# Graph network kernel: node update with fp16 halves and a new order of the engines' steps, and a re-ordered GCN stage

## The chip, the cores and the metric

One core of one Trainium2 chip. The metric is the device time of one execution in microseconds (us). The kernel is written in Bass: every engine's instruction stream, its waits and its semaphores are written out by hand.

## What is computed

Four graph layers on 10,000 nodes of 512 features (x) with 2,500 edges, each behind a layer norm and relu and each added to x:

```
x = x + GCN(h)       # h = relu(layernorm(x)); 512 -> 128 -> 512, symmetric degree weights, self loops
x = x + SAGE(h)      # 3 sublayers: relu(h @ Wself + mean(h[src]) @ Wneigh + b), rows scaled to unit length
x = x + MPNN(h)      # the layer with the node update that is changed
x = x + SAGEConv(h)  # mean aggregation, batch norm over the nodes, relu
```

The third layer, with mish(z) = z * tanh(softplus(z)):

```
h        = mish([x[src], x[dst], edge_attr] @ W1 + b1)
messages = mish(h @ W2 + b2)
agg      = segment_sum(messages, dst)
u        = mish([x, agg] @ W3 + b3)
y        = x + u @ W4 + b4
out      = layernorm(y) * gamma + beta
```

## The kernel before, in words

The rows live in SBUF for the whole run, in 79 tiles of 128 rows ("slots"). Nodes that receive edges sit in the last 20 tiles (t = 59 to 78, "the zone"), so that only these meet messages. Activations that feed a product are kept as two fp16 halves (high and low part of a scaled fp32), turned so that features lie on the partitions. A product with fp16 halves takes three matmuls per 128 features: high by high weight, low by high weight, high by low weight. A product with fp32 operands takes one matmul per 128 features, which the trace shows as two records.

The stages run one after the other, with barriers between them:

- **prepare** (lines 228 to 702, 0 to 197 us of the span): sorts the edges, and splits each weight matrix into fp16 halves. The matrices stand in the dictionary `units` (line 133): for each, SyncE loads it, VectorE takes its largest absolute value (L590), ScalarE makes the high half (L439), VectorE the low half (L629), SyncE stores both (L343). Then come the bias parts (L646 to L652, L348) and last one large store of the selection matrices (L350), on whose landing the barrier waits.
- **gcn_layer** (lines 789 to 1221, 197 to 614 us) works on pairs of tiles in 55 steps of one shared schedule. `of_rows(s, lag, ...)` does rows pair g = s - lag: gather x (POOL L921), moments (VectorE L762), factors (POOL L772 to L780), normalise (ScalarE L785), turn (TensorE), project 512 to 128 (TensorE L1155), turn back (L1162), write the rows (VectorE L1020 or L1026). The zone's ten pairs come first. `of_end(s, lag, ...)` does end pair q = s - 10 - lag: product with Wlin (TensorE L1198), residual and moments (VectorE L1053, L762), factors again, normalise, turn, make halves (ScalarE L1120, VectorE L1061). For the last ten pairs, the zone's, it first gathers the edges' rows (POOL L955), passes a running sum from tile to tile (`carry`: VectorE copy L1035, TensorE L1171), builds a diagonal (VectorE L1043) and convolves (TensorE L1183, L1185; ScalarE L1107). Each engine's order within a step is the order of its `of_rows` and `of_end` lines. From step 10 on POOL also issues two indirect DMAs per step for slot numbers (L932, L937), from step 31 on three for sources (L944).
- three **sage_layer** calls, **edge_hidden**, then **edge_messages** (lines 1799 to 1930, 1822 to 1978 us): 20 tiles of messages; VectorE's `totals` (L1881) scales the aggregated product with W3's lower half and SyncE stores it for the node update.
- **node_update** (lines 1962 to 2253, 1980 to 2636 us): 79 tiles in 40 pairs, see below.
- **batch_rows** and **finish** (lines 2263 to 2458).

In the node update, step s of every engine holds work of three pairs. `whole_pair(v, lag, ...)` and `of_pair(v, lag, ..., which)` pick pair s - lag and the tiles of it:

- TensorE: `update` of pair s (L2217 adds b3 with a 3-row matmul, L2221 are the 48 matmuls of 256 columns), `second` of pair s-1 tile 0 (L2230 adds b4, L2234 adds x, L2239 are four fp32 products with W4, eight records), `turn` of pair s-2 (L222, eight transposes), `second` of pair s-1 tile 1.
- ScalarE: `next_rows` of s-2 (L743, relu of the norm), sigmoid, log, tanh of pair s (L2167, two instructions of 512 columns each; mish is written as z * tanh(-ln(sigmoid(-z)))), with the copies `hi` of s-2 (L2195) between log and tanh.
- VectorE: `residual` (L2132 and moments L716) and `y_stats` (L716) of s-1 and s-2, `add_messages` of pair s (L2101, zone only), `lo` (L2140), `times_z` (L2110, two of 512 columns, makes u).
- POOL: factors of both norms and `add_beta` (L2055). SyncE: loads and stores.

u (the buffers `uT`) is fp32 and double-buffered by pair. The wait that ties TensorE to the others is `pe.wait_ge(s_u, 2 * v.g + 2)` ahead of L2239.

## Time and profile before

| | us |
|---|---|
| median of 3 runs | 3074.97 (3073.33 to 3088.87) |
| the profiled execution | 3073.27 |
| its span, first to last instruction | 3071.0 |
| TensorE busy | 2573.3 (84%) |
| VectorE busy | 1851.7 (60%) |
| ScalarE busy | 1505.4 (49%) |
| POOL busy | 1221.5 (40%) |
| granted TensorE clock, mean | 0.950 of 2.4 GHz |

Busy times are averages over stages with different limits. Times in the rows below are from the start of the span. In a timeline row the columns are: start in us, time from the first start to the last end of the merged group in us, engine, line and operation, output from input, shapes, count, and in brackets the idle time before it with what ended it. "issue" means that the engine waited for nothing that the profile shows.

### The profile page before, as it was taken

To read this page: it belongs to the slowest core of one execution; us is meant where nothing else is said; L and a number is where in the kernel's file an instruction comes from. 1 tells how busy PE (TensorE), PEld (TensorE's weight loads), DVE (VectorE), ACT (ScalarE), POOL (GpSimd) and SP (SyncE) were. 2 spreads that over 40 slices of the span, in tenths; PEclk is the share of its full clock that TensorE was granted. 3 is DMA by queue.
4 is the path that set the end of the run, shared out by engine and by line. 5 is a ranking of instruction groups with operands and counts; after the bars stand their busy time and mean duration, and the time that the engine had idled before them with its cause. 6 is when DMAs were issued, how large, how long until landed. Compare 5 with 4: busy or idle time off the path is not lost. (4 is left out here: it accounts for less than half of the span.)

```text
span 3071.0 us, 44367 instructions
## 1 busy us (share of the span) xinstructions
PE 2573.3 (84%) x13170; PEld 1453.0 (47%) x13170; DVE 1851.7 (60%) x4344; ACT 1505.4 (49%) x2128; POOL 1221.5 (40%) x2065
## 2 busy tenths in 40 slices
PE   0347888789887999798979969799999999899964
PEld 0234554344443445344544547565555555444443
DVE  8744876578666876799864435345555566423333
ACT  7235665345333533355335756466666666332270
POOL 3666874236332332365545511133333333100146
PEclk9999998899998999899989989899999999999976
DMA  5154442278766887666553322322222234101268
GB/s 173 59 213 124 150 145 92 78 184 201 134 123 156 203 171 152 192 221 220 181 182 105 101 80 85 103 81 95 96 99 102 89 134 138 71 1 38 57 225 312
DMA packets 379160, 412.03 MB, mean 134 GB/s; under 512 B 198351, under 2 KB 237683, under 8 KB 376316
## 3 DMA queue, kind: packets, MB, share of 16 engines
q1 hardware_dynamic: 350364, 335.34, 37.0%
q0 software_dynamic: 28640, 74.78, 8.1%
q8 instruction: 78, 1.28, 0.2%
q14 instruction: 78, 0.64, 0.1%
HBM read 171.50 MB, written 197.28 MB: 120 GB/s over the span
## 5 line engine op out<-in xcount | busy, mean ns | idle before, releaser
L215 PE MATMUL s_ps_z<-s_w,slots 128*128 128x512 f16 x2844 | 645.7, 384 | 41.7 <-DMA s_bias<-in_L_gnn_b 41.7
L215 PEld LDWEIGHTS s_ps_z<-s_w,slots 128*128 128x128 f16 (+1 forms) x2844 | 280.9, 99 | 363.3 <-DMA s_bias<-in_L_gnn_b 43.1
L1571 ACT ACTIVATE s_g<-s_g,s_rn 128x512 f32<-128x512 f32 x237 | 170.0, 717 | 287.7 <-POOL s_rn L1461 287.7
L2239 PE MATMUL u_ps_o<-u_w,u_uT 128*128 128x512 f32 x632 | 288.6, 599 | 0.2 <-DVE u_uT L2110 0.2
L1461 POOL TENSOR_TENSOR s_rn<-s_em,minus_half 128x1 f32<-128x1 f32 x237 | 179.6, 758 | 253.0 <-DVE s_em L1515 245.1
L1500 DVE SCALAR_TENSOR_TENSOR s_g<-s_ps_z,s_f,s_bias 128x512 f32<-128x512 f32 x237 | 177.9, 751 | 140.3 <-PE s_ps_z L215 132.0
L2221 PE MATMUL u_ps_z<-slots,u_w 128*128 (+2 forms) x1920 | 236.7, 273 | 0.0
L2349 PE MATMUL z_ps_z<-slots,z_w 128*128 128x512 f16 (+1 forms) x960 | 211.7, 380 | 7.2 <-DMA z_w<-split_root 7.2
L2221 PEld LDWEIGHTS u_ps_z<-slots,u_w 128*128 128x128 f16 x1920 | 173.9, 98 | 37.7 <-issue 0.4
L716 DVE BATCH_NORM_STATS2 u_ny_st<-u_ps_o 128x6 f32<-128x512 f32 x79 | 54.7, 692 | 213.7 <-PE u_ps_o L2239 213.7
L743 ACT ACTIVATE u_h<-u_x,u_n_sh,u_n_rs 128x512 f32<-128x512 f32 x79 | 64.3, 814 | 229.3 <-POOL u_n_sh L738 229.3
L2239 PEld LDWEIGHTS u_ps_o<-u_w,u_uT 128*128 128x128 f32 x632 | 113.9, 190 | 113.7 <-issue 113.3
L1508 DVE SCALAR_TENSOR_TENSOR s_junk<-s_g 128x512 f32<-128x512 f32 x237 | 164.5, 694 | 4.1
L2167 ACT ACT_TABLE_LOAD x120 | 154.0, 1283 | 26.3 <-PE u_ps_z L2221 24.1
L215 PE MATMUL s_ps_z<-s_wn,s_aT 128*128 128x512 f16 x720 | 165.2, 379 | 0.0
L2318 DVE BATCH_NORM_STATS2 z_stats<-slots 128x6 f32<-128x512 f32 (+1 forms) x76 | 52.2, 687 | 185.7 <-ACT slots L2335 185.7
L743 ACT ACTIVATE s_h<-s_x,s_norm_sh,s_norm_rs 128x512 f32<-128x512 f32 x79 | 64.2, 813 | 176.0 <-POOL s_norm_sh L738 95.9
L2349 PEld LDWEIGHTS z_ps_z<-slots,z_w 128*128 128x128 f16 x960 | 94.6, 99 | 116.0 <-DMA z_w<-split_root 7.6
L2335 ACT ACTIVATE slots<-z_ps_z,bn_cols,z_f 128x512 f32<-128x512 f32 (+1 forms) x76 | 58.7, 772 | 158.3 <-PE z_ps_z L2349 158.2
L1292 POOL DMA_INDIRECT z_m<-h_rows,src_s x20 | 19.0, 950 | 257.1 <-DVE z_aT L1338 251.7
L215 PEld LDWEIGHTS s_ps_z<-s_wn,s_aT 128*128 128x128 f16 x720 | 70.4, 98 | 85.0
L1526 DVE SCALAR_TENSOR_TENSOR s_halves<-s_g,s_halves 128x512 f16<-128x512 f32 x158 | 108.0, 684 | 2.5 <-ACT s_halves L1559 2.5
(370 smaller groups left out, 5445.0 us busy)
## 6 DMA issues: line engine op xcount, KB each, us to landing
h_rows<-s_g SPq DMA_DIRECT2D x158, 256.0 KB
x_rows<-q_x SPq DMA_DIRECT2D x79, 256.0 KB
s_x<-x_rows SPq DMA_DIRECT2D x79, 256.0 KB
x_rows<-s_x SPq DMA_DIRECT2D x79, 256.0 KB
h_rows<-s_h SPq DMA_DIRECT2D x79, 256.0 KB
u_x<-x_rows SPq DMA_DIRECT2D x79, 256.0 KB
x_rows<-u_x SPq DMA_DIRECT2D x79, 256.0 KB
h_rows<-u_h SPq DMA_DIRECT2D x79, 256.0 KB
```

Source lines behind the costliest of these rows:

```text
L215: ins = nc.tensor.matmul(out_ap, a(c), w[:, part * size + c * n:part * size + (c + 1) * n], start=first and c == 0 and m == 0, stop=stop a ...
L743: return nc.scalar.activation(out_ap, in_ap, func, scale=self.rstd[b][:, 0:1], bias=self.shift[b][:, 0:1])
L1461: nc.gpsimd.tensor_tensor(out=rn[b][:, :], in0=em[b][:, :], in1=minus_half[:, :], op=POW).then_inc(s_rn, 1)
L1500: nc.vector.scalar_tensor_tensor(out=g[b][:, :], in0=ps_z[v.buf(4)][:, :], scalar=f[:, 0:1], in1=bias[:, :], op0=MUL, op1=ADD).then_inc(s_ ...
L1508: nc.vector.scalar_tensor_tensor(out=junk[:, :], in0=r[:, :], scalar=0.0, in1=r[:, :], op0=MAX, op1=MUL, accum_out=en[e][:, 0:1]).then_inc ...
L1526: nc.vector.scalar_tensor_tensor(out=part[:, D:2 * D], in0=g[v.buf(ng)][:, :], scalar=scale_out, in1=part[:, 0:D], op0=MUL, op1=SUB).then_ ...
L1571: nc.scalar.activation(g[b][:, :], g[b][:, :], ACT.Relu, scale=rn[v.buf(2)][:, 0:1]).then_inc(s_h, 1)
L2167: nc.scalar.activation(part, z if first else part, func, scale=scale, **kw).then_inc(sem, 1)
L2221: ins = nc.tensor.matmul(z, w3[:, at:at + P], pair_slots[:, :, part * D + k * P:part * D + (k + 1) * P], start=False, stop=k == C - 1 and ...
L2239: ins = nc.tensor.matmul(ps_o[b][:, :], ut_tile(v, c), w4[:, c * D:(c + 1) * D], start=False, stop=c == C - 1)
L2335: nc.scalar.activation(z_of(zx, g, c)[:, 0:n], ps_z[c][:, 0:n], ACT.Identity, scale=f[:, 0:1], bias=bn_cols[:, c:c + 1]).then_inc(s_z, 1)
L2349: ins = nc.tensor.matmul(out_ap, weights[:, at:at + P], a(k), start=first and k == 0 and m == 0, stop=stop and k == C - 1 and m == 2)
```

## The change

It splits W4 into fp16 halves like the other weights, and multiplies by them:

```diff
-    bias_d = dram("bias_parts", [3, 2 * D], BF16)
+    bias_d = dram("bias_parts", [3, D], BF16)
-    units = {"conv": (Wc, 1), "edge": (W1[0:2 * D, :], 2), "update": (W3[0:D, :], 1),
+    units = {"conv": (Wc, 1), "edge": (W1[0:2 * D, :], 2), "update": (W3[0:D, :], 1), "out": (W4, 1),
...
-                for k, v in enumerate((bl, gamma3, beta3)):
+                for k, v in enumerate((bl, gamma3, beta3, b3)):
```

In gcn_layer, epsilon is added by VectorE, the end pairs run one step later with four `cT` buffers, the zone's rows are scaled a second time when they are written, and the diagonal is gone:

```diff
-        def factors(self, pool, g, n, done, s_used, used, consts):
+        def above_eps(self, dve, g, n, done):
             b = g % 2
-            pool.wait_ge(self.s_mv, done)
-            nc.gpsimd.tensor_tensor(out=self.nm[b][:, 0:n], in0=self.mv[b][:, 0:n, 0], in1=minus_one2, op=MUL)
-            nc.gpsimd.tensor_tensor(out=self.ve[b][:, 0:n], in0=self.mv[b][:, 0:n, 1], in1=eps2, op=ADD).then_inc(
-                self.s_ve, 1)
+            dve.wait_ge(self.s_mv, done)
+            nc.vector.tensor_scalar(out=self.ve[b][:, 0:n], in0=self.mv[b][:, 0:n, 1], scalar1=LN_EPS, scalar2=None,
+                                    op0=ADD).then_inc(self.s_ve, 1)
+
+        def factors(self, pool, g, n, s_used, used, minus_one2, minus_half2):
+            b = g % 2
             pool.wait_ge(self.s_ve, g + 1)
+            nc.gpsimd.tensor_tensor(out=self.nm[b][:, 0:n], in0=self.mv[b][:, 0:n, 0], in1=minus_one2[:, 0:n], op=MUL)
...
-        FINISH = 3
+        FINISH = 4
...
                         ins.then_inc(s_rows, 1)
+                        dve.wait_ge(s_rows, g + 1)
+                        for k in range(2):
+                            e = 2 * g + k
+                            nc.vector.tensor_scalar(out=hwz[:, e * HID:(e + 1) * HID], in0=hw[g % 2][:, k * HID:(k + 1) * HID],
+                                                    scalar1=dis_dst[:, e:e + 1], scalar2=None, op0=MUL).then_inc(s_hwz, 1)
...
                 for s in range(STEPS):
-                    of_end(s, FINISH, lambda q: carry(q, 0))
-                    of_end(s, FINISH, lambda q: diagonal(q, 0))
-                    of_end(s, FINISH, lambda q: carry(q, 1))
                     of_end(s, FINISH + 2, lo)
                     of_rows(s, 0, lambda g: moments(g, 0))
                     of_rows(s, 2, rows_out)
                     of_rows(s, 0, lambda g: moments(g, 1))
-                    of_end(s, FINISH, lambda q: diagonal(q, 1))
                     of_end(s, FINISH, lambda q: residual(q, 0))
+                    of_end(s, FINISH - 1, lambda q: carry(q, 0))
                     of_end(s, FINISH, lambda q: residual(q, 1))
+                    of_end(s, FINISH - 1, lambda q: carry(q, 1))
...
-                        nc.tensor.matmul(out_ap, hwz[:, e * HID:(e + 1) * HID], diag[e % 2][:, :], start=True, stop=False)
+                        nc.tensor.matmul(out_ap, hwz[:, e * HID:(e + 1) * HID], ident[:, :], start=True, stop=False)
...
                     of_rows(s, 2, project)
-                    of_end(s, FINISH, lambda q: carry(q, 0))
                     of_rows(s, 1, lambda g: turn(g, 0))
                     of_end(s, FINISH, lambda q: convolve(q, 0))
                     of_rows(s, 1, lambda g: turn(g, 1))
-                    of_end(s, FINISH, lambda q: carry(q, 1))
                     of_rows(s, 2, rows)
                     of_end(s, FINISH, lambda q: convolve(q, 1))
                     of_end(s, FINISH, lambda q: linear(q, 0))
                     of_end(s, FINISH + 1, lambda q: turn1(q, 0))
                     of_end(s, FINISH, lambda q: linear(q, 1))
+                    of_end(s, FINISH - 1, lambda q: carry(q, 0))
                     of_end(s, FINISH + 1, lambda q: turn1(q, 1))
+                    of_end(s, FINISH - 1, lambda q: carry(q, 1))
```

edge_messages also takes the largest absolute message sum of each tile, and runs VectorE's loop unrolled:

```diff
+                    wait_count(dve, s_zmax, v.t - 1)
                     nc.vector.tensor_scalar(out=tot[b][:, :], in0=ps_g[b][:, :], scalar1=scale[:, 0:1],
                                             scalar2=None, op0=MUL).then_inc(s_tot, 1)
+                    dve.wait_ge(s_tot, v.t + 1)
+                    nc.vector.tensor_reduce(out=z_max[:, v.t:v.t + 1], in_=tot[b][:, :], op=MAX, axis=AX.X,
+                                            apply_absolute_value=True).then_inc(s_zmax, 1)
...
-                         (0, lambda v: mish.result(dve, r[:, :], v)), peel=8)
+                         (0, lambda v: mish.result(dve, r[:, :], v)), peel=ET, loop_end=ET)
```

In node_update some twenty small VectorE instructions and one small matmul at its start work out a power of two `g` for u from these maxima and b3. Then, per pair (`uT` is now one buffer, `u_hi` and `u_lo` are one fp16 buffer each, `unscale` is bf16; the three `step` functions below are those of VectorE, ScalarE and TensorE; `centred` is `y_stats` together with L2126, until now the first instruction of `residual`; `load_sigmoid_and_tanh` loads the one table set of ScalarE that holds both functions):

```diff
-                def times_z(k):
-                    def stage(v, tiles):
...
-                        nc.vector.tensor_tensor(out=part, in0=z, in1=part, op=MUL).then_inc(s_u, 1)
+                def times_z(v, tiles):
+                    for c in range(C):
+                        dve.wait_ge(s_th, mish_count(v, c // 2))
+                        part = chunk(uT, c, tiles)
+                        ins = nc.vector.scalar_tensor_tensor(out=part, in0=z_chunk(v, c, tiles), scalar=b3_cols[:, c:c + 1],
+                                                             in1=part, op0=ADD, op1=MUL)
+                        if c % 2:
+                            ins.then_inc(s_u, 1)
+                def lo_u(k):
+                    def stage(v, tiles):
+                        dve.wait_ge(s_uhi, mish_count(v, k))
+                        nc.vector.scalar_tensor_tensor(out=half(u_lo, k, tiles), in0=half(uT, k, tiles), scalar=g[:, 0:1],
+                                                       in1=half(u_hi, k, tiles), op0=MUL, op1=SUB).then_inc(s_ulo, 1)
+                    return stage
-                def y_stats(v):
+                def centred(v):
...
                 def step(v):
-                    of_pair(v, 2, residual, (1,))
-                    of_pair(v, 0, add_messages(0))
-                    of_pair(v, 0, add_messages(1))
-                    of_pair(v, 1, y_stats, (0,))
+                    of_pair(v, 1, centred, (0,))
+                    whole_pair(v, 0, times_z)
+                    whole_pair(v, 0, lo_u(0))
+                    whole_pair(v, 0, lo_u(1))
                     of_pair(v, 1, residual, (0,))
+                    of_pair(v, 1, centred, (1,))
+                    of_pair(v, -1, add_messages(0))
+                    of_pair(v, -1, add_messages(1))
                     of_pair(v, 2, lo)
-                    whole_pair(v, 0, times_z(0))
-                    whole_pair(v, 0, times_z(1))
-                    of_pair(v, 1, y_stats, (1,))
+                    of_pair(v, 1, residual, (1,))
...
+                def sigmoid(k):
+                    def stage(v, tiles):
+                        z_there(v, k)
+                        wait_count(act, s_ulo, mish_count(v, k) - 2)
+                        for c in (2 * k, 2 * k + 1):
+                            ins = nc.scalar.activation(chunk(uT, c, tiles), z_chunk(v, c, tiles), ACT.Sigmoid,
+                                                       scale=minus_f[:, 0:1], bias=minus_b3[:, c:c + 1])
+                        ins.then_inc(s_s, 1)
+                    return stage
+                def tanh(v, tiles):
+                    load_sigmoid_and_tanh(act)
...
+                def hi_u(v, tiles):
+                    wait_count(act, s_mm4, v.t)
+                    for k in range(2):
+                        act.wait_ge(s_u, mish_count(v, k))
+                        nc.scalar.activation(half(u_hi, k, tiles), half(uT, k, tiles), ACT.Copy,
+                                             scale=g[:, 0:1]).then_inc(s_uhi, 1)
                 def step(v):
-                    of_pair(v, 2, next_rows)
-                    whole_pair(v, 0, sigmoid)
+                    whole_pair(v, 0, sigmoid(0))
+                    of_pair(v, 2, next_rows, (0,))
+                    whole_pair(v, 0, sigmoid(1))
                     whole_pair(v, 0, log)
+                    whole_pair(v, 0, tanh)
+                    of_pair(v, 2, next_rows, (1,))
+                    whole_pair(v, 0, hi_u)
                     of_pair(v, 2, hi)
-                    whole_pair(v, 0, tanh)
...
-                        nc.tensor.matmul(z, b3_rows[:, c * P:(c + 1) * P], ones3[:, 0:tiles * P], start=True, stop=False)
...
-                    pe.wait_ge(s_u, 2 * v.g + 2)
+                    pe.wait_ge(s_uhi, 2 * v.g + 2)
+                    for part in range(2):
+                        for c in range(C):
+                            nc.tensor.matmul(ps_o[b][:, :], chunk_of_tile(u_hi, v, c),
+                                             w4[:, part * cols["out"] + c * D:part * cols["out"] + (c + 1) * D],
+                                             start=False, stop=False)
+                    pe.wait_ge(s_ulo, 2 * v.g + 2)
                     for c in range(C):
-                        ins = nc.tensor.matmul(ps_o[b][:, :], ut_tile(v, c), w4[:, c * D:(c + 1) * D],
+                        ins = nc.tensor.matmul(ps_o[b][:, :], chunk_of_tile(u_lo, v, c), w4[:, c * D:(c + 1) * D],
                                                start=False, stop=c == C - 1)
                 def step(v):
                     whole_pair(v, 0, update)
-                    of_pair(v, 1, second, (0,))
+                    of_pair(v, 1, second)
                     of_pair(v, 2, turn)
-                    of_pair(v, 1, second, (1,))
```

POOL's step becomes y_factor tile 0, add_beta, h_factors tile 0, y_factor tile 1, h_factors tile 1, all of pair s-1.

## Rows read from the trace of the kernel before

**Rows 1.** Windows: busy us of each engine, TensorE clock, DMA share, GB/s

```profile
2100.00:2600.00 500.00, 500.00 (x2923) 296.65 (x2922) 287.74 (x656) 315.97 (x404) 188.79 (x439) 1.00 0.31 107
290.00:420.00 130.00, 113.39 (x527) 68.23 (x528) 102.49 (x278) 90.43 (x150) 106.75 (x196) 1.00 0.48 148
530.00:614.00 84.00, 59.41 (x228) 30.95 (x226) 47.07 (x124) 29.95 (x54) 25.27 (x50) 0.85 0.23 79
```

**Rows 2.** Waits from 2100 to 2600 us: total us, times, longest

```profile
DVE u_ny_st L716 <- PE u_ps_o L2239: 169.1, 31, 6.2
```

**Rows 3.** Timeline of the node update, TensorE, one step of a pair

```profile
2304.44 0.28 PE L2217 MATMUL u_ps_z<-u_ones,u_b_rows 3*128 3x256 bf16 x1
...
2306.28 1.48 PE L2221 MATMUL u_ps_z<-slots,u_w 128*128 x12
...
2310.95 0.39 PE L2230 MATMUL u_ps_o<-u_b_rows,u_ones 3*128 3x512 bf16 x1
...
2311.72 3.65 PE L2239 MATMUL u_ps_o<-u_w,u_uT 128*128 128x512 f32 x8
...
2315.21 1.04 PE L222 MATMUL u_ps_t<-ident,u_h 128*128 128x128 f32 x8
...
2316.18 0.39 PE L2230 MATMUL u_ps_o<-u_b_rows,u_ones 3*128 3x512 bf16 x1
...
2320.54 0.28 PE L2217 MATMUL u_ps_z<-u_ones,u_b_rows 3*128 3x256 bf16 x1
```

**Rows 4.** Timeline of batch_rows, TensorE, fp16 matmuls of 512 columns

```profile
2699.76 16.57 PE L2349 MATMUL z_ps_z<-slots,z_w 128*128 128x512 f16 x76
```

**Rows 5.** Timeline of the node update, ScalarE

```profile
2312.66 1.26 ACT L2167 ACTIVATE u_uT<-u_ps_z,u_minus_f 128x512 f32<-128x512 f32 x2
...
2313.94 1.28 ACT L2167 ACT_TABLE_LOAD   x1
...
2315.24 1.34 ACT L2167 ACTIVATE u_uT<-u_uT,floor_col 128x512 f32<-128x512 f32 x2
...
2316.48 1.06 ACT L2195 ACTIVATE slots<-u_ps_t 128x512 f32 x2
...
2318.85 1.15 ACT L2167 ACTIVATE u_uT<-u_uT 128x512 f32<-128x512 f32 x2
...
2326.61 0.81 ACT L743 ACTIVATE u_h<-u_x,u_n_sh,u_n_rs 128x512 f32<-128x512 f32 x1 [5.16 <-POOL u_n_sh L738]
```

**Rows 6.** Timeline of the node update, VectorE

```profile
2301.41 0.75 DVE L2132 SCALAR_TENSOR_TENSOR u_x<-u_ps_o,u_ny_rs,u_x 128x512 f32<-128x512 f32 x1 [0.27 <-POOL u_ny_rs L2065]
...
2550.22 0.74 DVE L2101 TENSOR_TENSOR u_ps_z<-u_ps_z,u_zg 128x256 f32<-128x256 f32 x2
```

**Rows 7.** Timeline of prepare and of edge_messages, VectorE

```profile
94.54 24.75 DVE L590 TENSOR_REDUCE w_mx<-slots 128x1 f32<-128x512 f32 x11
...
176.95 4.68 DVE L629 SCALAR_TENSOR_TENSOR w_parts<-slots,up,w_parts 128x2048 f16<-128x2048 f32 x2 [2.73 <-ACT w_parts L439]
...
1882.72 1.12 DVE L1254 SCALAR_TENSOR_TENSOR n_total<-n_carry_w,n_carry_on,n_ps_a 128x128 f32<-128x128 f32 x4 [2.11 <-PE n_ps_a L1916]
```

**Rows 8.** Timeline of gcn_layer, POOL, one step with gathers

```profile
382.33 0.22 POOL L773 TENSOR_TENSOR q_norm_ve<-q_norm_mv,q_eps 128x2 f32<-128x2 f32 x1
382.63 0.72 POOL L777 TENSOR_TENSOR q_norm_rs<-q_norm_ve,q_minus_half 128x2 f32<-128x2 f32 x1
...
390.52 0.72 POOL L777 TENSOR_TENSOR q_norm_rs<-q_norm_ve,q_minus_half 128x2 f32<-128x2 f32 x1
```

**Rows 9.** Timeline of gcn_layer, VectorE, the zone's end pairs

```profile
514.07 0.17 DVE L1037 MEMSET q_m<- 1x128 f32 x1 [4.50 <-DMA q_m<-projection_rows,src_s]
...
569.66 0.26 DVE L1035 COPY q_m<-q_ps_t 1x128 f32<-1x128 f32 x1
...
580.81 0.26 DVE L1035 COPY q_m<-q_ps_t 1x128 f32<-1x128 f32 x1
...
588.88 0.26 DVE L1035 COPY q_m<-q_ps_t 1x128 f32<-1x128 f32 x1
```

More of the change, by code:

```diff
@@ L47 @@
 SIGMOID_FLOOR = 2.0 ** -80
+SIGMOID_AND_TANH = 2
 PEEL = 12
@@ L828, in gcn_layer @@
             sl = [sb(ctx, f"q_sel{b}", [P, P]) for b in range(4)]
-            diag = [sb(ctx, f"q_diag{b}", [P, P]) for b in range(2)]
             bias_row = x1[0][0:1, :]
@@ L2156, in _ @@
             def _(act):
-                act.wait_ge(s_f, 2)
-                def each_half(sem, before, func, scale, bias=None, first=False):
-                    def stage(v, tiles):
-                        b = v.j // 2
-                        for k in range(2):
-                            before(v, k)
-                            part = uT[b][:, k * D:(k + 1) * D].rearrange("p (c n) -> p c n", c=2)[:, :, 0:tiles * P]
-                            z = ps_z[b][k][:, :].rearrange("p (c n) -> p c n", c=2)[:, :, 0:tiles * P]
-                            kw = {} if bias is None else {"bias": bias}
-                            nc.scalar.activation(part, z if first else part, func, scale=scale, **kw).then_inc(sem, 1)
-                    return stage
+                act.wait_ge(s_f, 1)
@@ L2182, in _ @@
-                sigmoid = each_half(s_s, z_there, ACT.Sigmoid, minus_f[:, 0:1], first=True)
-                log = each_half(s_l, s_there, ACT.Ln, 1.0, bias=floor_col[:, 0:1])
-                tanh = each_half(s_th, l_there, ACT.Tanh, -1.0)
+                def sigmoid(k):
[7 more added lines that the diff above has]
+                    return stage
@@ new lines, in log @@
+                def log(v, tiles):
+                    for k in range(2):
+                        act.wait_ge(s_s, mish_count(v, k))
+                        nc.scalar.activation(half(uT, k, tiles), half(uT, k, tiles), ACT.Ln, scale=1.0,
+                                             bias=floor_col[:, 0:1]).then_inc(s_l, 1)
+                def tanh(v, tiles):
+                    load_sigmoid_and_tanh(act)
+                    for k in range(2):
+                        act.wait_ge(s_l, mish_count(v, k))
+                        nc.scalar.activation(half(uT, k, tiles), half(uT, k, tiles), ACT.Tanh, scale=-1.0).then_inc(s_th, 1)
```

233 lines of the change are left out of this document (130 added, 103 removed).

## The prediction

> **What bounds the kernel now.** The windows come first. In the node update TensorE is busy 500.00 of 500.00 us at full clock, while VectorE has 287.74, ScalarE 315.97 and POOL 188.79; in gcn_layer no engine is full (PE 113.39, DVE 102.49, ACT 90.43, POOL 106.75 of 130) and in its last part none is near (59.41 of 84, at clock 0.85) [rows 1]. The waits agree: what VectorE waits for in the node update is TensorE's L2239, 169.1 us in that window [rows 2]. So there TensorE's own work sets the time. The timeline gives it per pair: from one L2217 at 2304.44 to the next at 2320.54 is 16.10 us, made of the update 6.51, `second` 4.26, turn 0.97 and `second` 4.36 [rows 3]. In GCN the step is a chain through several engines.
>
> I sum against the profiled execution's own 3073.27 us, 1.7 below the median; the two stand for the same kernel.
>
> **Node update, TensorE.** In the update a chunk takes 6.51 / 4 = 1.63 us, its bias matmul included, while the 12 matmuls alone run from 2306.28 for 1.48 [rows 3]. Taking a last matmul of 0.27 off, 11 gaps make 1.21, so 0.11 each and 12 x 0.11 = 1.32. Without the bias a chunk saves 1.63 - 1.32 = 0.31, a pair 1.24, and the update is 5.27. In `second`, eight fp32 records fill the tile's end at 0.43 each = 3.44. They become 12 fp16 matmuls of 512 columns. The kernel has such a run elsewhere: 76 in 16.57 us, (16.57 - 0.38) / 75 = 0.216 each [rows 4], so 2.59; a tile saves 0.85. The pair step becomes 5.27 + 3.41 + 3.51 + 0.97 = 13.2. Over 40 updates and 79 seconds this is 49.6 + 67 = **-117**. It counts only while the others keep pace.
>
> **ScalarE, hand schedule.** Let 0 be the end of `second` of the pair before. The halves of u wait for it: hi_u two instructions like `hi` (1.06 for two [rows 5]; 1.3 with their strided input, my estimate) to 1.6, `hi` to 2.7. The next update's first half is ready at 0.97 + 2.64 = 3.6; sigmoid is now four instructions of 256 columns, about 0.95 per half against 1.26 for two of 512 [rows 5], started at 3.95, with a relu (0.81 [rows 5]) between, and ends at 7.55. Then load 1.30 with its gap (2313.94 to 2315.24), log 1.34, load 1.30, tanh 1.15 [rows 5]: 12.65. The second relu ends at 13.5; TensorE wants it for the turn at about 13.75. ScalarE is thus busy some 11 of 13.2 us, on a chain with 0.3 us to spare. It holds only because the third load of a pair goes.
>
> **VectorE.** lo_u 2 x 0.7, residual 0.75 [rows 6], centred and lo end by 9.1; centred of the next tile waits for `second` at about 9.7, and times_z (four, from the 0.37 of a 256-column add [rows 6], 0.42 with a column operand) ends near 13.9. Busy 12.2 of 13.2. The first half's u is there for hi_u by then, and `second` doesn't use it for 5 us more. No stall.
>
> **The zone's ten pairs.** add_messages of pair s+1 (0.74 per half [rows 6]) now stands behind centred(s-1, 1) on VectorE, which ends near 6.1. So ScalarE's sigmoid starts near 7 instead of 3.95, and its chain no longer fits: the second relu ends at 15.5, the step is about 15.2, 2.0 more than 13.2. **10 x 2.0 = +20**, the late item being next_rows tile 1, TensorE's turn behind it. Filling the pipeline: the first `second` waits some 8 us for mish after the first update where the second update covers 5.3, **+2.5**. The 20 small VectorE links at the start (0.2 each, like L773's kind of operation [rows 8]) run beside the weights' loading, on which TensorE waits anyhow: nothing, or 20 x 0.25 = 5 if not covered. POOL's new order and its 188.79 of 500 [rows 1] leave it idle more than half of a 13.2 step. Stage: -117 + 20 + 2.5, about **-94**.
>
> **GCN.** Epsilon leaves POOL: a step there is L777 to L777, 7.89 us, in which L773 takes 0.22 and its wait as much again [rows 8]. I take 7.6, not 7.3: from rows_out on, VectorE's next scalings and residual of the same step hold it there (an estimate; 7.3 and 7.89 are the ends). Sixteen steps with gathers x 0.3 = -4.8; five with sources too x 0.6 = -3; three at 0.3, -0.9. In the first eight steps, where VectorE writes the zone's rows, two more scalings and a wait cost +0.5 each, +4. One more pipeline step (FINISH = 4), a short one at the end, +4.2, my estimate between nothing and one zone step of 8.07. SyncE's load of the selections stays one step ahead of its use, and its store of the rows, now in two queues, waits only for VectorE's first scaling. The first edge gather's wait of 4.50 [rows 9] now lies beside other work, -4.3. In the zone's end pairs, carry and diagonal leave the chain: 8.07 (580.81 to 588.88) falls to about 7.0, and the slow one, 569.66 to 580.81 = 11.15 [rows 9] at half clock, to less; 8.07 is what most take, three of nine were slow, mean 9.1, and I expect the same share slow: 10 x 1.2 = -12. One more VectorE add of 0.2 a step is in these. Together **-17**; from -30 (these steps no longer sag in clock) to 0 (the chain was not theirs).
>
> **Prepare.** One more matrix of 2048 columns: L590's eleven reduces take 24.75, 2.2 per 2048 columns; its low half is one L629 more, 4.68 / 2 = 2.35 [rows 7]; the bias parts lose one instruction of 0.26. VectorE is what SyncE's last stores, bias parts and selections, wait for: **+4.3**. SyncE issues one load of a matrix more; it lies beside VectorE's earlier reduces, so nothing. Range 2 to 8.
>
> **edge_messages.** Twenty reduces of 0.7 plus a wait on VectorE, where it idles 2.11 us a tile for TensorE [rows 7]: nothing. If that cover is gone, 20 x 0.85 = +17.
>
> Sum: -94 - 17 + 4.3 = -107, so **2966**.
>
> **Rivals.**
> *A, ScalarE's chain is late.* The slack of 0.3 us is less than my errors, and if the third load stays (or the sigmoids of 256 columns, or a semaphore hop at each engine change, cost 1 us more than I say) the turn waits 1.1 us per pair: 38 x 1.1 = +42, **3005**. For it: the step's long serial chain. Against: today ScalarE idles for a third of the time. 0.2.
> *B, no stall in the zone and GCN gains its full range.* If the sum sits in front of TensorE's need: -20 and -10, **2938**. 0.14.
> *C, slower.* TensorE now gets gaps. GCN's last stretch, in which it idles, ran at clock 0.85 [rows 1], and a step took 11.15 there where another took 8.07 [rows 9]. If the node update falls from the 2.4 GHz level to 1.2, a step goes from 13.2 to about 26. From 107 / 13.2 = 8 of the 40 steps on it eats the gain; twelve give 2966 + 158 = **3124**, all 3490. Against: TensorE would still work in nearly all of each step outside the zone, and in the zone 13.2 of 15.2. 0.02.
> *D, a table load holds ScalarE for longer than the 1.30 of rows 5*, where nothing follows it at once: another 1.3, as much as its own length. Two a pair on a chain with no slack make the step 15.8, 38 x 2.6 = +99, **3065**. Rows 5 speak against it: the log starts 1.30 after its load began, in the very order that stays. 0.02. The Trainium skill ("ScalarE: Activation LUTs", § What ACT_TABLE_LOAD costs) has such a rule: a switch of table set costs the load of 1283 ns and then a drain of about 1380. By it this rival's time would hold; the trace shows the load's 1.28 and not the drain.
> *E, the mixed types slow `second`.* Unscale becomes bf16 against fp16 rows. No row shows that mix. At the least it costs nothing: eight fp16 pieces take 2311.72 - 2310.95 - 0.32 for the bias = 0.45, or 0.056 each [rows 3]. At the most it runs like fp32 pieces of that width, the transposes' (2316.18 - 2315.21) / 8 = 0.12 [rows 3], and twice over: (0.24 - 0.056) x 16 = 2.9 a pair, 2966 + 116 = **3082**. I take nothing, since both types have 16 bits. 0.02.
>
> **Numbers.** My case 0.6, A 0.2, B 0.14, C, D and E 0.02 each. That the third load stays, so that the change does not do what it says, is in A. The range takes my case with GCN's ends, B and A: 2938 to 3008. About 0.5%, 15 us, is what a measurement of this kernel can tell from no change. Faster by more: 0.6 + 0.2 + 0.14 = 0.94; D and E end within it (3065, 3082), same 0.04; C, slower 0.02.
>
> **What would show it.** Two table loads per pair, not three; no L2217; `second`'s last matmuls 0.216 apart; pair steps of 13.2 outside the zone and about 15.2 in it; the relu of tile 1 ending just before the turn; GCN steps of 7.6 with gathers, 7.0 in the zone; prepare's end 4.3 later. Wrong if TensorE shows idle time before the turn or `second` outside the zone (A, D), if its clock falls below 1.00 there (C), or if the unscaling matmuls grow (E).

## The result

The changed kernel takes **2974.86 us** (median of 4 executions, 2966.35 to 2975.68) against 3076.84 (4 executions). The ratio is 0.9656 (95% interval 0.9624 to 0.9688): **faster by 3.4%**. The forecast was 2966, so it was 9 us too low, inside its range. The profiled execution took 2975.29 us, its span is 2973.6.

By stages, from one stage's first instruction to the next one's, in the two profiled executions:

| stage | before | after | difference | forecast |
|---|---|---|---|---|
| prepare | 197.5 | 209.4 | +11.9 | +4.3 |
| gcn_layer | 417.7 | 398.0 | -19.7 | -17 |
| sage_layer x3, edge_hidden | 1187.8 | 1189.3 | +1.5 | 0 |
| edge_messages | 177.3 | 178.1 | +0.8 | 0 |
| node_update | 663.6 | 567.3 | **-96.3** | -94 |
| batch_rows, finish | 427.2 | 431.4 | +4.2 | 0 |

(Stages here start at an engine's first instruction on one of the stage's own buffers; batch_rows at TensorE's first product.)

### The profile page after: what moved, and what is told of

Same layout as the page of the kernel before. It is cut to its first block and busy times, and to the rows that moved or that the text cites. A ratio compares the mean times of both kernels' runs of the same rounds, so it can differ in the third digit from the quotient of the medians.

```text
span 2973.6 us, 45046 instructions
## 1 busy us (share of the span) xinstructions
PE 2450.1 (82%) x13328; PEld 1425.9 (48%) x13328; DVE 1950.1 (66%) x4623; ACT 1531.0 (51%) x2250; POOL 1195.6 (40%) x1984
## 5 line engine op out<-in xcount | busy, mean ns | idle before, releaser
L2294 PE MATMUL u_ps_z<-slots,u_w 128*128 (+2 forms) x1920 | 215.6, 273 | 0.0
L2294 PEld LDWEIGHTS u_ps_z<-slots,u_w 128*128 128x128 f16 x1920 | 187.0, 98 | 22.2
L2313 PE MATMUL u_ps_o<-u_w,u_hi 128*128 128x512 f16 x632 | 149.3, 379 | 2.0 <-ACT u_hi L2253 2.0
L2232 ACT ACTIVATE u_uT<-u_ps_z,u_minus_b,u_minus_f 128x256 f32<-128x256 f32 (+1 forms) x160 | 80.9, 557 | 76.1 <-PE u_ps_z L2294 68.3
L733 POOL TENSOR_TENSOR u_n_nm<-u_n_mv,minus_one 128x1 f32<-128x1 f32 x79 | 15.0, 190 | 240.6 <-DVE u_n_mv L727 240.6
L790 ACT ACTIVATE q_h<-slots,q_norm_sh,q_norm_rs 128x512 f32<-128x512 f32 x79 | 60.0, 805 | 96.0 <-POOL q_norm_sh L785 63.4
L217 PE MATMUL e_ps<-e_w,e_hT 128*128 128x512 f16 x480 | 107.1, 379 | 0.0
```

The costliest lines, as they stand in the source:

```text
L217: ins = nc.tensor.matmul(out_ap, a(c), w[:, part * size + c * n:part * size + (c + 1) * n], start=first and c == 0 and m == 0, stop=stop a ...
L790: return nc.scalar.activation(out_ap, in_ap, ACT.Relu, scale=self.rstd[b][:, k:k + 1], bias=self.shift[b][:, k:k + 1])
L2232: ins = nc.scalar.activation(chunk(uT, c, tiles), z_chunk(v, c, tiles), ACT.Sigmoid, scale=minus_f[:, 0:1], bias=minus_b3[:, c:c + 1])
L2294: ins = nc.tensor.matmul(z, w3[:, at:at + P], pair_slots[:, :, part * D + k * P:part * D + (k + 1) * P], start=k == 0 and m == 0, stop=k = ...
L2313: nc.tensor.matmul(ps_o[b][:, :], chunk_of_tile(u_hi, v, c), w4[:, part * cols["out"] + c * D:part * cols["out"] + (c + 1) * D], start=Fal ...
```

## The profile after

The first row of the changed kernel's page (busy times and instructions):

```profile
PE 2450.1 (82%) x13328; PEld 1425.9 (48%) x13328; DVE 1950.1 (66%) x4623; ACT 1531.0 (51%) x2250; POOL 1195.6 (40%) x1984
```

Its windows of the node update outside the zone and in it, and of GCN's last stretch; the columns are as in [rows 1]:

```profile
2100.00:2400.00 300.00, 297.94 (x2243) 202.26 (x2242) 244.79 (x558) 245.81 (x364) 135.58 (x321) 1.00 0.36 126
2410.00:2500.00 90.00, 82.45 (x604) 54.18 (x602) 73.61 (x176) 66.40 (x101) 35.68 (x84) 1.00 0.44 146
535.00:595.00 60.00, 49.00 (x225) 24.34 (x224) 42.72 (x116) 24.90 (x49) 23.63 (x42) 0.99 0.33 112
```

Outside the zone TensorE is still busy 297.94 of 300 us at full clock, beside 244.79 of VectorE and 245.81 of ScalarE, which per microsecond are 42% and 30% more than in [rows 1] (0.82 against 0.58, 0.82 against 0.63). In the zone it is busy 82.45 of 90. Two of the changed kernel's waits from 2100 to 2400 us (total, times, longest):

```profile
DVE u_ny_st L719 <- PE u_ps_o L2318: 25.2, 21, 1.3
...
ACT u_h L746 <- POOL u_n_sh L741: 14.0, 20, 0.7
```

And one from 2410 to 2500 us, in the zone:

```profile
PE u_ps_t L228 <- ACT u_h L746: 7.5, 6, 1.5
```

VectorE's wait for TensorE, 169.1 us of 500 in [rows 2], is 25.2 of 300. In the zone a new one stands there: TensorE's turn waits for ScalarE's relu, 7.5 us over 6 pairs.

One step of TensorE outside the zone, the answer to [rows 3]:

```profile
2230.43 5.40 PE L2294 MATMUL u_ps_z<-slots,u_w 128*128 x48
2235.76 0.38 PE L2304 MATMUL u_ps_o<-u_b_rows,u_ones 3*128 3x512 bf16 x1
...
2236.54 1.89 PE L2313 MATMUL u_ps_o<-u_w,u_hi 128*128 128x512 f16 x8
2238.27 1.03 PE L2318 MATMUL u_ps_o<-u_w,u_lo 128*128 128x512 f16 x4
2239.22 0.38 PE L2304 MATMUL u_ps_o<-u_b_rows,u_ones 3*128 3x512 bf16 x1
...
2242.59 1.04 PE L228 MATMUL u_ps_t<-ident,u_h 128*128 128x128 f32 x8
2243.46 0.71 PE L2294 MATMUL u_ps_z<-slots,u_w 128*128 x5
```

The step is 2243.46 - 2230.43 = 13.03 us: the update 5.33, `second` 3.46 and 3.37, turn 0.87. No L2217 stands between the chunks, and W4 takes twelve fp16 matmuls. Nothing idles. The timeline of ScalarE in the same step of the changed kernel:

```profile
2229.76 1.33 ACT L2253 ACTIVATE u_hi<-u_uT,u_g 128x512 f16<-128x512 f32 x2
...
2233.33 1.02 ACT L2232 ACTIVATE u_uT<-u_ps_z,u_minus_b,u_minus_f 128x256 f32<-128x256 f32 x2 [1.27 <-PE u_ps_z L2294]
2235.02 0.81 ACT L746 ACTIVATE u_h<-u_x,u_n_sh,u_n_rs 128x512 f32<-128x512 f32 x1 [0.67 <-POOL u_n_sh L741]
...
2238.20 1.33 ACT L2240 ACTIVATE u_uT<-u_uT,floor_col 128x512 f32<-128x512 f32 x2
2239.55 1.28 ACT L223 ACT_TABLE_LOAD   x1
2240.85 1.15 ACT L2247 ACTIVATE u_uT<-u_uT 128x512 f32<-128x512 f32 x2
2241.90 0.80 ACT L746 ACTIVATE u_h<-u_x,u_n_sh,u_n_rs 128x512 f32<-128x512 f32 x1
```

In a zone step of the same trace, ScalarE's first sigmoid:

```profile
2438.50 1.02 ACT L2232 ACTIVATE u_uT<-u_ps_z,u_minus_b,u_minus_f 128x256 f32<-128x256 f32 x2 [4.13 <-PE u_ps_z L2294]
```

VectorE's additions of the messages before it:

```profile
2437.35 1.65 DVE L2155 TENSOR_TENSOR u_ps_z<-u_ps_z,u_zg 128x256 f32<-128x256 f32 x4
```

And TensorE, with the second tile's turn of the step before:

```profile
2432.23 0.66 PE L228 MATMUL u_ps_t<-ident,u_h 128*128 128x128 f32 x4 [1.21 <-ACT u_h L746]
```

Two table loads a pair (81 in the stage for its 40 pairs, 120 before), and the chain of the prediction in its order: hi_u 2229.76, sigmoid 2233.33, log 2238.20, tanh 2240.85, relu 2241.90, and the next hi_u at 2242.79. In the zone the sigmoid idles 4.13 us and starts only when VectorE has done the first half's message additions (2437.35, behind L2185, the last instruction of centred), and TensorE's turn idles 1.21 us between its first and its second tile. The row puts the sigmoid's wait down to TensorE; that it is the additions shows in e4, where they stand earlier and the sigmoid follows the update's start by 4.2 us (2418.69 to 2422.87) and not by 5.8 (2432.72 to 2438.50). Nine of the last ten steps took 14.45 to 14.77 us and one 14.11, the forecast was 15.2.

## The experiments

All were compared with the kernel before on the same chip. The stage times are those of the profiled execution, counted as in the table above. Eight profiled executions with the changed gcn_layer (the changed kernel's own, e1 and e3 to e8) give 391.5 to 400.4 for that stage, mean 396.6. So a single stage time of GCN says little about less than some 5 us; its zone steps repeat far better (6.77 us in all eight).

### e1, the changed gcn_layer alone; e2, all but the changed gcn_layer

```diff
e1:  (the kernel before)
-    class PairNorm, def gcn_layer: before
+    class PairNorm, def gcn_layer: changed
e2:  (the changed kernel)
-    class PairNorm, def gcn_layer: changed
+    class PairNorm, def gcn_layer: before
```

> The kernel before with the changed gcn_layer alone; nothing else of the change. If the two halves of the change add up, GCN gives its 20 us (the stage from 417.7 to about 398) and the time is about 3077 - 20 = 3057. The node update's pair step stays 16.1 and prepare ends at 197 to 198, because prepare has no new matrix. Rival: the 20 us came from somewhere else in the profile (the other gathers, the clock), then the stage takes 410 or more and the time is over 3065. For prepare: in the changed kernel it ended 7.6 us later than the new matrix explains. If that is the state of one execution and not the change, this run may end at 197 or up to 205.

> The changed kernel with gcn_layer as before. Theory: the node update gives all of its 98 us without it: time about 2975 + 20 = 2995, pair step 13.0, zone step 14.5; in GCN the zone's steps are 8.07 again with some at 11.15. Prepare is the changed one: 201.8 (197.5 + 4.3) if the 7.6 us were chance, 209.4 again if they belong to the new matrix.

e1: 3064.71 us, ratio 0.9934 (0.9910 to 0.9958). GCN 396.3, node update 663.6 as before, prepare 203.4. e2: 2997.54 us, ratio 0.9718 (0.9698 to 0.9738). GCN 420.4, node update 567.9, prepare 208.1. 0.9934 x 0.9718 = 0.9654, and the whole change has 0.9656: **the two parts add up**, and each gives what it gives in the whole.

Prepare doesn't fit either theory as a fixed cost. With the new matrix it ended at 209.4 in the changed kernel and at 208.1, 210.1, 203.5, 204.0, 200.3, 204.5, 204.2, 200.2, 199.9 and 200.1 in e2 to e11, without it at 197.5 (before) and 203.4 (e1). The stall can be read in the changed kernel, where ScalarE and VectorE both wait for the same turn of TensorE; in the page's words the releaser is "remote", which is to say none that the trace shows (timeline of ScalarE, prepare):

```profile
137.11 0.17 ACT L436 ACTIVATE carry_c<-g_ps_sel 128x1 f32<-128x1 f32 x1 [4.82 <-remote]
...
144.18 0.17 ACT L436 ACTIVATE carry_c<-g_ps_sel 128x1 f32<-128x1 f32 x1 [5.61 <-remote]
```

4.82 and 5.61 us are idle there; the row of before at 133.84 has 2.86. In e9 no turn waits for longer than 1.48:

```profile
134.47 0.17 ACT L436 ACTIVATE carry_c<-g_ps_sel 128x1 f32<-128x1 f32 x1 [1.04 <-PE g_ps_sel L701]
```

Twenty such copies (L436, in the old prepare L432) stand in prepare, one for each of the zone's tiles. Their idle time adds up to 20.1 us in the changed kernel, 12.7 in before, 18.0 in e1 and 10.9 in e9 to e11. Taken off the end of prepare, it leaves 189.0 to 189.5 in all eleven executions with the new matrix, and 184.8 and 185.4 in the two without. **So the new matrix costs 4.1 us on the mean**, and 7.4 of the 11.9 is the difference of the stalls (20.1 - 12.7), an execution's chance. What delays the signal was not found.

### e3, three table loads again

```diff
                 def tanh(v, tiles):
-                    load_sigmoid_and_tanh(act)
```

> The changed kernel without the hand-placed table load, so that tanh and sigmoid each get a load of their own as before: three loads a pair. Theory: ScalarE's chain has no slack (the relu of the second tile ended at 2242.70, the turn's second half could only then go on), so the load of 1.28 lies bare in every step: 13.0 becomes 14.2 to 14.3, 40 x 1.28 = +51 at most, about +45 us, near 3020. Rival: the chain has slack of a microsecond (TensorE showed no idle time): less than +15 us, step under 13.4.

2992.37 us, ratio 0.9704 (0.9681 to 0.9726), some +15 us on the changed kernel and not +45; the node update takes 586.7, +19.4. The steps alternate between 13.2 and 13.3 outside the zone, and are 15.3 to 16.1 in it. **The theory fell outside the zone.** ScalarE's timeline of e3 shows why:

```profile
2216.92 1.28 ACT L2232 ACT_TABLE_LOAD   x1 [1.38 <-PE u_ps_z L2293]
2218.22 1.02 ACT L2232 ACTIVATE u_uT<-u_ps_z,u_minus_b,u_minus_f 128x256 f32<-128x256 f32 x2
```

The relus of e3 from 2100 to 2400 us, as a group of its instructions by line (busy, mean ns, idle before):

```profile
L746 ACT ACTIVATE u_h<-u_x,u_n_sh,u_n_rs 128x512 f32<-128x512 f32 x45 | 36.1, 803 | 0.5 <-POOL u_n_sh L741 0.5
```

In the changed kernel the relu of the first tile, between the two sigmoids, waits 14.0 us, 20 times, for POOL's factors (0.67 at 2235.02). The load pushes it back, and that wait becomes 0.5 in all. 1.28 - 0.67 = 0.61 is left, and only 0.25 of it reaches the step (13.25 for 13.0), so by subtraction the rest of the chain takes up the other 0.36. The chain had a slack of 1.28 - 0.25 = 1.0, most of it in its middle, where the prediction's serial sum (0.3) had not looked. In the zone that relu has no wait in the changed kernel either, and 1.2 of the 1.28 reaches the step.

Each load again costs its own length: 2216.92 to 2218.22 is 1.30, like the 1.30 of [rows 5].

### e4 and e8, the zone's additions ahead of centred

```diff
                     of_pair(v, 1, residual, (0,))
-                    of_pair(v, 1, centred, (1,))
                     of_pair(v, -1, add_messages(0))
+                    of_pair(v, 1, centred, (1,))
                     of_pair(v, -1, add_messages(1))
```

> The changed kernel, but VectorE adds the messages of the next pair's first half ahead of centred of the second tile. Theory: in the zone the sigmoid waited for the two message additions behind centred (2438.50 instead of 2436.6 or so), and this is all of the 1.5 us by which a zone step (14.5) is longer than the others (13.0). Then the zone's step falls to 13.0 to 13.4 and the time by 11 to 15 us, about 2962. Rival: ScalarE or TensorE is held by something else there (the loads of the message totals, the second half's addition): step 14.0 or more, less than 5 us.

> The order of e4 once more beside the changed kernel: its zone steps were 13.7 against 14.5, ten of them, so 8 us (0.26%) under e7. Rival: no difference that a measurement can tell, under 3 us.

> The changed kernel itself beside the others on the same chip, to compare with e8 and to see what of prepare's 209.4 is chance. Theory: 0.966 of before; prepare ends anywhere from 203 to 210, by waits on the semaphores of TensorE that no engine's work fills.

e4: 2968.20 us, ratio 0.9634 (0.9616 to 0.9652). On another chip, side by side: e7, the changed kernel, 2962.89, 0.9620 (0.9596 to 0.9644); e8 2957.46, 0.9607 (0.9585 to 0.9630). The medians are 5.4 us apart, and the intervals overlap, so the whole time doesn't tell the two apart. The stage does: 559.6 and 559.4 against 567.3 and 568.0, **8 us less**, zone steps of 13.7 for 14.5.

The additions on VectorE's timeline in a zone step of e4:

```profile
2421.73 0.74 DVE L2155 TENSOR_TENSOR u_ps_z<-u_ps_z,u_zg 128x256 f32<-128x256 f32 x2
...
2424.20 0.77 DVE L2155 TENSOR_TENSOR u_ps_z<-u_ps_z,u_zg 128x256 f32<-128x256 f32 x2
```

Its two sigmoids on ScalarE:

```profile
2422.87 1.02 ACT L2232 ACTIVATE u_uT<-u_ps_z,u_minus_b,u_minus_f 128x256 f32<-128x256 f32 x2 [2.53 <-issue]
...
2425.05 1.02 ACT L2232 ACTIVATE u_uT<-u_ps_z,u_minus_b,u_minus_f 128x256 f32<-128x256 f32 x2 [0.46 <-issue]
```

And what TensorE's turn still waits:

```profile
2431.94 0.66 PE L228 MATMUL u_ps_t<-ident,u_h 128*128 128x128 f32 x4 [0.48 <-ACT u_h L746]
```

The first half's additions are done at 2422.47, ahead of centred, and the sigmoid starts at 2422.87 (by the code's waits; the row names no releaser). A zone step takes 13.74 for 14.46: 0.7 of the 1.4 us are gone, against 1.1 to 1.5 expected. What is left stands at the second half: the update's second half is done only near 2424.1, its addition ends at 2424.97, and the second sigmoid starts at 2425.05 after 0.46 of idle time. TensorE's turn still waits 0.48. That these two are all of the rest was not tested. This version is the fastest of those tried.

### e5, the halves with the old order

```diff
                 def step(v):
+                    of_pair(v, 2, next_rows)
                     whole_pair(v, 0, sigmoid(0))
-                    of_pair(v, 2, next_rows, (0,))
                     whole_pair(v, 0, sigmoid(1))
                     whole_pair(v, 0, log)
+                    of_pair(v, 2, hi)
                     whole_pair(v, 0, tanh)
-                    of_pair(v, 2, next_rows, (1,))
                     whole_pair(v, 0, hi_u)
-                    of_pair(v, 2, hi)
```

VectorE, POOL and TensorE get the order of before too, with lo_u last on VectorE. The folded bias, the single `uT` and L2185 as a part of centred stay as in the changed kernel, and the place of lo_u is a choice: so e5 is one old-order schedule with the halves, not the only one.

> The changed kernel with its fp16 halves, but with each engine's step of the node update in the order of before (hi_u behind tanh, lo_u last on VectorE). Theory: TensorE's own work stays 13.0 a pair, but ScalarE's chain from one hi_u to the next then takes sigmoid (waits for the whole update's half), two loads, log, hi, which waits for the turn behind the first second, tanh, times_z and hi_u, about 14.6. So the step is 14.4 to 15 and the time about 2980 + 60 = 3040. Rival: the order is worth little and the halves are everything: step under 13.4, under +15 us.

3049.52 us, ratio 0.9897 (0.9871 to 0.9924). The node update takes 653.4, only 10 us less than before and **86 more than with the new order**. A pair takes (2579.4 - 1974.9) / 39 = 15.5 us on average, in a pattern from 13.0 to 19.0; 14.4 to 15 were expected.

One of e5's waits from 2100 to 2400 us:

```profile
ACT u_h L746 <- POOL u_n_sh L741: 83.6, 19, 4.4
```

TensorE's timeline of e5 behind one of these:

```profile
2242.59 0.99 PE L228 MATMUL u_ps_t<-ident,u_h 128*128 128x128 f32 x4 [2.29 <-ACT u_h L746]
...
2244.05 1.03 PE L2306 MATMUL u_ps_o<-u_unscale,slots 128*128 128x128 bf16 x8
2244.87 2.54 PE L2312 MATMUL u_ps_o<-u_w,u_hi 128*128 128x512 f16 x8
```

And the window of e5 over the same 300 us:

```profile
2100.00:2400.00 300.00, 267.27 (x1862) 173.73 (x1862) 201.47 (x460) 206.08 (x305) 114.97 (x267) 0.95 0.29 100
```

The direction was right, the place only in part: what ScalarE waits longest for is POOL's factors ahead of the relu (83.6 us, 4.4 at a time); these stand behind VectorE's residual (2238.69), and that behind lo_u (2237.36). And there is a second cost that I had not counted: after TensorE's gap of 2.29 us the granted clock is 0.50 from 2242.8 to 2246.1, the 1.2 GHz level. The eight unscaling matmuls take 1.03 instead of 0.62, L2312 2.54 instead of 1.89, and the 300 us window's granted clock is 0.95.

### e6, W4 in fp32 with the new order

```diff
-                    pe.wait_ge(s_uhi, 2 * v.g + 2)
...
+                    pe.wait_ge(s_u, 2 * v.g + 2)
                     for c in range(C):
-                        ins = nc.tensor.matmul(ps_o[b][:, :], chunk_of_tile(u_lo, v, c), w4[:, c * D:(c + 1) * D],
+                        ins = nc.tensor.matmul(ps_o[b][:, :], chunk_of_tile(uT2[v.j // 2], v, c), w4[:, c * D:(c + 1) * D],
                                                start=False, stop=c == C - 1)
```

> The changed kernel with its new order and b3 on ScalarE and VectorE, but with the second product in fp32 as before (W4 is loaded in fp32, scaled once, u double-buffered, no hi_u and lo_u). Theory by TensorE's rows: update 5.33, two seconds of 4.26, turn 0.87: step 14.7, which is 1.7 above 13.0: the halves alone are worth 40 x 1.7 = 68 us, time about 3045. Rival: the new order was tuned for the halves and the step is 16 again, time near 3090.

3012.01 us, ratio 0.9779 (0.9755 to 0.9804). The step is 14.8 everywhere, in the zone as well, and the node update takes 614.9.

TensorE's timeline of e6 at three places of a step, its two `second` and the next update:

```profile
2234.83 0.39 PE L2289 MATMUL u_ps_o<-u_b_rows,u_ones 3*128 3x512 bf16 x1
...
2239.19 0.39 PE L2289 MATMUL u_ps_o<-u_b_rows,u_ones 3*128 3x512 bf16 x1
...
2244.32 1.91 PE L2279 MATMUL u_ps_z<-slots,u_w 128*128 x16
```

The step was as forecast (14.7); the total was not, 3012 for 3045. My expectation had let all 40 pairs gain 1.7, but in the zone the fp32 version doesn't stall (14.83) and the fp16 one does, so that the last ten steps gain 3.7 together (148.3 to 144.6). The 26 steps outside the zone gain 26 x 1.8 = 46.8, the first three, where the pipeline fills, 1.3, and behind the last update e6 is 4.4 shorter: 47.4, which is the stage's 48 but for rounding. **Folded bias and new order without the halves: 663.6 to 614.9, -49. The halves on top: 614.9 to 567.3, -48.** The prediction's terms were -49.6 for the bias, -67 for the halves and +20 for the zone. The bias folded in with the old order and the fp32 product was not run, so what the -49 needs of the order is open.

### e9 to e11, the three parts of GCN's change undone one by one

```diff
e9:
+            nc.gpsimd.tensor_tensor(out=self.ve[b][:, 0:n], in0=self.mv[b][:, 0:n, 1], in1=eps2[:, 0:n], op=ADD).then_inc(
+                self.s_ve, 1)
             pool.wait_ge(self.s_ve, g + 1)
e10:
+                    of_end(s, FINISH, lambda q: diagonal(q, 0))
                     of_end(s, FINISH + 2, lo)
...
+                    of_end(s, FINISH, lambda q: diagonal(q, 1))
                     of_end(s, FINISH, lambda q: residual(q, 0))
e11:
-                    of_end(s, FINISH - 1, lambda q: carry(q, 0))
-                    of_end(s, FINISH - 1, lambda q: carry(q, 1))
+                    of_end(s, FINISH, lambda q: carry(q, 0))
+                    of_end(s, FINISH, lambda q: carry(q, 1))
```

> The changed kernel with epsilon added by POOL again, as before, in gcn_layer. Theory: where POOL with its gathers holds the step (steps 13 to 29) 7.35 and 7.68 in turn go back to 7.9 or a little less; +0.35 x 16 = +6 us in the stage (398 to 404). In the zone's end pairs POOL has little to do, but epsilon is on the chain from moments to factors: +0.3 a step, 6.77 to 7.1. Rival: POOL was not the bound there, the gain came from the step added (FINISH = 4): no change in the gather steps.

> The changed kernel with the diagonal again: VectorE builds it per tile, the zone's rows are copied instead of scaled a second time, all else as changed. Theory: the diagonals are two instructions of 0.3 on VectorE's chain in the zone's end pairs: 6.77 becomes 7.0 to 7.4, +5 us. Rival: the diagonal was the costly part and the step is back near 8.07 with some at half clock.

> The changed kernel with the carries of a pair in the step that convolves it, as before (VectorE and TensorE), all else as changed. Theory: the two carries (copy, matmul, copy, matmul, each with its semaphores, some 1 us each) come back in front of convolve: 6.77 becomes 7.7 to 8.1, and the stage takes 10 to 20 us more, the more if TensorE's clock falls to 1.2 GHz in some steps as before. Rival: they lay beside other work: under 7.0.

Each was executed once, so only the stage counts, and in it the steps: **e9 407.2, e10 415.4, e11 410.6** against 396.6. One instruction of POOL's timeline, L782 (L783 in e9), comes once a step. In steps with gathers of the changed kernel:

```profile
396.12 0.74 POOL L782 TENSOR_TENSOR q_norm_rs<-q_norm_ve,q_minus_half 128x2 f32<-128x2 f32 x1
...
403.46 0.74 POOL L782 TENSOR_TENSOR q_norm_rs<-q_norm_ve,q_minus_half 128x2 f32<-128x2 f32 x1
...
411.15 0.74 POOL L782 TENSOR_TENSOR q_norm_rs<-q_norm_ve,q_minus_half 128x2 f32<-128x2 f32 x1
```

The same of e9:

```profile
399.24 0.72 POOL L783 TENSOR_TENSOR q_norm_rs<-q_norm_ve,q_minus_half 128x2 f32<-128x2 f32 x1
...
407.14 0.72 POOL L783 TENSOR_TENSOR q_norm_rs<-q_norm_ve,q_minus_half 128x2 f32<-128x2 f32 x1
```

In the zone's end pairs, the changed kernel:

```profile
587.40 0.72 POOL L782 TENSOR_TENSOR q_norm_rs<-q_norm_ve,q_minus_half 128x2 f32<-128x2 f32 x1
...
594.16 0.69 POOL L782 TENSOR_TENSOR q_norm_rs<-q_norm_ve,q_minus_half 128x2 f32<-128x2 f32 x1
```

e9:

```profile
587.66 0.72 POOL L783 TENSOR_TENSOR q_norm_rs<-q_norm_ve,q_minus_half 128x2 f32<-128x2 f32 x1
...
594.22 0.69 POOL L783 TENSOR_TENSOR q_norm_rs<-q_norm_ve,q_minus_half 128x2 f32<-128x2 f32 x1
```

e10, with the diagonal:

```profile
584.31 0.73 POOL L782 TENSOR_TENSOR q_norm_rs<-q_norm_ve,q_minus_half 128x2 f32<-128x2 f32 x1
...
592.00 0.72 POOL L782 TENSOR_TENSOR q_norm_rs<-q_norm_ve,q_minus_half 128x2 f32<-128x2 f32 x1
...
601.27 0.69 POOL L782 TENSOR_TENSOR q_norm_rs<-q_norm_ve,q_minus_half 128x2 f32<-128x2 f32 x1
```

e11, with the carries in their own step:

```profile
588.01 0.72 POOL L782 TENSOR_TENSOR q_norm_rs<-q_norm_ve,q_minus_half 128x2 f32<-128x2 f32 x1
...
595.28 0.69 POOL L782 TENSOR_TENSOR q_norm_rs<-q_norm_ve,q_minus_half 128x2 f32<-128x2 f32 x1
...
604.15 0.69 POOL L782 TENSOR_TENSOR q_norm_rs<-q_norm_ve,q_minus_half 128x2 f32<-128x2 f32 x1
```

Epsilon: the steps with gathers are 7.69 and 7.34 in turn, mean 7.51, and 7.90 with it back on POOL, so 0.39 each, 6.2 in the sixteen steps; the following ones, with the sources' gathers too, take 4.2 more. The rival is out. In the zone it is the other way round: 6.56 with epsilon on POOL, 6.77 with it on VectorE, which is the fuller of the two there (42.72 of 60 us busy against POOL's 23.63).

Diagonal: 7.69, and every second step 9.27. Carry: 7.28, and two of eight 8.87, where 7.7 to 8.1 was expected. In both the long steps go with a lower clock. The window of e10 over 535 to 595 us has 0.90 for it,

```profile
535.00:595.00 60.00, 46.93 (x184) 22.79 (x184) 36.86 (x105) 22.57 (x44) 20.67 (x35) 0.90 0.27 92
```

and in e11 0.94, where the changed kernel has 0.99, and the kernel before has one step of three at 11.1 [rows 9]. The theory for e10 had 7.0 to 7.4 and missed both the size and the clock; its rival had the clock. So the diagonal is the dearest of the three in the zone (eight steps take 66.2 us with it, 61.4 with the carries back, 54.2 in the changed kernel), and either of the two was enough by itself to bring slow steps back. Undoing them costs 19 and 14 us, with epsilon's 10.6 some 43 together, while the whole change gives 20 to 24 (417.7 in before and 420.4 in e2 against 396.6). A likely reason is that what they share is counted twice, and that the added pipeline step and the second scaling (5.45 to 5.90 us in the eight steps where the zone's rows are written) are paid out of the gain; no two parts were undone together, so this is not shown.

## Why the prediction was right

**Bound.** TensorE's own work sets the node update, before and after: right. No rival's stall stands outside the zone.

**TensorE's terms.** Update 5.33 for 5.27, `second` 3.46 and 3.37 for 3.41 and 3.51, turn 0.87 for 0.97, step 13.03 for 13.2, or 39 steps x 3.07 = 120 for the -117. The price from [rows 4] holds: from 2240.00 to 2242.59 twelve matmuls take 2.59, 0.216 each. **Rival E** (mixed types) is out: L2307 with bf16 takes 0.62, as L2234 did with fp16.

**ScalarE's chain.** The hand schedule's end came out within 0.4 us (the relu of tile 1 ends at 2242.70, 13.1 us after the end of `second`, forecast 13.5), its slack did not: e3 measured 1.0 us, the prediction had 0.3. **Rival A** was priced at +42 for 1.1 us of lateness, which makes 3008 as in the range, not the 3005 beside it; the third load alone, 1.28, brings 19.4, so its price was too high.

**Zone.** The mechanism was right: add_messages behind centred, the turn as the late item. The step is 14.5, not 15.2, and the mis-sized term is VectorE's (its forecast of 12.2 us busy in a step of 13.2 was too high as well: 244.79 of 300 us are 10.6 of 13.03). From the first sigmoid (2423.73) to the end of the second relu (2432.18) ScalarE takes 8.45, the schedule had 8.5. But from the end of the relu before (2417.71), over hi_u, lo_u, residual, centred and the additions, to that sigmoid it is 6.0, where the schedule had 6.7; 6.0 + 8.45 is the step. So the last ten steps take 144.6 us for 130.3 without the stall, 14.3 for the +20. In its place the start and the end of the stage cost more: the first three steps take 36.6 us against 39.8 before, 3.2 less where three full ones would save 3 x 3.07 = 9.2, so filling costs 6 and not 2.5, and what lies ahead of the first and behind the last update takes 3.1 more, which the prediction had at nothing. That -120 + 14.3 + 6 + 3.1 comes within 3 us of the forecast is in part luck: two of the terms came out better than forecast and two worse.

**GCN.** Steps with gathers 7.51 for 7.6, rows-only 5.90 for 5.95, zone 6.77 for 7.0. The failed step is "I expect the same share slow": none was, the last nine steps run at full clock. That gave some 23 us there (83.8 to 60.9) for the forecast 12. The steps ahead of the zone gave 2.2 for 4.7, and the start of the zone with the added step cost 5.4 (29.9 to 35.3, at a granted clock of 0.81), where the first edge gather's -4.3 and the added step's +4.2 had made it nothing. Together -19.7 for -17: here too errors of both signs met. **Rival B**, 2938, would have needed the whole of it and no stall; the zone stall stayed. (Its -20 and -10 make 2936, and with GCN's own end of -30 it would be 2933, not 2938; the measured time is far from all three.)

**Prepare and edge_messages.** The reduces and the low half cost what [rows 7] say (26.94 for twelve, one more L636 of 2.35), and over all runs the matrix costs 4.1 for the forecast 4.3; the rest of the +11.9 is chance, as e1 to e11 show. The twenty reduces of edge_messages, as a group of the changed kernel's instructions by line:

```profile
L1885 DVE TENSOR_REDUCE z_max<-n_tot 128x1 f32<-128x512 f32 x20 | 13.7, 686 | 0.7
```

take 13.7 us out of VectorE's idle time, which in front of L1254 still comes to 39.3 us; the stage grew by 0.8.

**Rivals C and D.** TensorE's clock stays 1.00 outside the zone. That C's mechanism exists e5 shows, where gaps of up to 2.3 us a step came with 0.95 and with stretches at the 1.2 GHz level. In the zone, with gaps of 1.2 to 1.5, the 90 us window still has 1.00. For D no row speaks: tanh starts at 2240.85 after the load at 2239.55. The Trainium skill ("ScalarE: Activation LUTs", § What ACT_TABLE_LOAD costs) has the load's 1283 ns, with which this trace agrees, and 1380 ns more of drain, which none of the rows here show; the measurement decides.

The 9 us between forecast and median are therefore no term of the change: the profiled execution has 7.6 in prepare and 5.7 in stages that the change doesn't touch, and 0.8 in edge_messages, against 2.3 and 2.7 that the node update and GCN gave beyond the forecast; and the executions of e7 gave 2962.89, beside 3080.53 for before.

## What to carry to other kernels

When TensorE bounds a stage, count its columns: a bias folded into an activation, with the order to go with it, and an fp32 product split into fp16 halves were worth 49 and 48 us here. But the halves brought two more instructions a pair on ScalarE and two on VectorE, and in the old order of e5 bias and halves together gave 10 us of the 96: the order of each queue can be the larger part of such a change and has to be worked out with it. And where a schedule is drawn by hand, list the waits inside the chain as well as its length, since they are slack that a sum of durations hides.

## What the runs showed that I had not expected

- The third table load (1.28 us, 39 times more: 120 loads for 81) cost 0.25 us a step outside the zone and 1.2 in it, for the same code.
- The same addition of epsilon costs 0.39 us a step on POOL while that engine issues gathers, and is 0.21 cheaper there than on VectorE in the zone's end pairs.
- GCN's zone steps ran at full clock at 6.77 us; at 7.28 two of eight, at 7.69 every second, and at 8.07 every third was slow. The slow ones took 1.6 us more in the first two cases and 3.1 at 8.07. So in e11 half a microsecond (6.77 to 7.28) cost 7.2 us in eight steps and not 4.1.
- In prepare, engines sat idle for up to 7.5 us (e3) before a signal whose sender had finished by the trace; the end of the stage moved by up to 10 us between executions of the same instructions (199.9 to 210.1), and with these waits taken off by 0.5.
